# Key logarithms added to the decay exponents, and two VectorE steps moved to ScalarE, in the first mixer of a two-layer network

## What is computed

```python
xc = silu(causal_conv4(x, conv_w))
q, kg, v, g = xc @ wq, xc @ wkg, xc @ wv, xc @ wg + bg
gk = log_sigmoid(kg) / 16
k = 1 - exp(gk)
S = S * exp(gk_t) + k_t (x) v_t        # for each token and head
o_t = (q_t * scale) S
o = o + sigmoid(sum(q * aug * k) * v)
o = head_norm(o)
x1 = layernorm(x + silu(g) * o @ wout)
```

## Time and profile before

| what | value |
|---|---|
| median of 3 runs | 4582.89 us (4578.5 to 4586.45) |
| the profiled execution's own time | 4581.29 us |
| its span | 4579.3 us |
| mean granted TensorE clock | 0.924 |
| span of the first mixer, from the slices and the last logits' copy | 0 to about 860 us |
| busy in the whole span: PE, PEld, DVE, ACT, POOL | 87%, 67%, 54%, 43%, 24% |

### The profile page before, as it was taken

The page is one execution under the profiler, slowest core; times in us unless marked ns, Lnnn a source line. Parts: engine busy times, 40 slices in busy tenths (PEclk is TensorE's granted clock), DMA queues, the critical chain, the costliest instruction groups (busy, mean ns, idle before and its releaser), DMA issues. The chain is left out here.

```text
span 4579.3 us, 72621 instructions
## 1 busy us (share of the span) xinstructions
PE 3966.9 (87%) x23860; PEld 3077.2 (67%) x23860; DVE 2462.0 (54%) x5456; ACT 1990.2 (43%) x4069; POOL 1085.3 (24%) x1689
## 2 busy tenths in 40 slices
PE   5887788698999999993798888888888888769998
PEld 3555555377888888881576767676767677646666
DVE  7888888452222222224577777777777676421111
ACT  5655655111222222212466666666666566432222
POOL 0111111102222222212343333333333332200000
PEclk8888888799999999996799999999999999879999
DMA  1010010345555555552111111111111110011111
GB/s 34 29 42 28 28 42 20 75 135 179 183 183 183 184 183 185 183 170 68 39 42 40 43 41 42 42 42 38 42 43 42 42 42 25 20 51 55 55 55 46
DMA packets 220427, 345.91 MB, mean 76 GB/s; under 512 B 99956, under 2 KB 171380, under 8 KB 201972
## 3 DMA queue, kind: packets, MB, share of 16 engines
q1 hardware_dynamic: 196404, 271.69, 18.7%
q0 software_dynamic: 23760, 71.07, 4.9%
HBM read 275.56 MB, written 67.63 MB: 75 GB/s over the span
## 5 line engine op out<-in xcount | busy, mean ns | idle before, releaser
L525 ACT ACTIVATE moe_rel<-moe_fc 128x512 f32<-128x512 f32 x284 | 169.6, 597 | 798.5 <-PE moe_fc L490 798.5
L490 PE MATMUL moe_fc<-moe_xT,moe_win 128*128 128x256 f32 x2272 | 503.8, 380 | 1.5 <-issue 0.8
L501 PE MATMUL moe_o<-moe_wout,moe_hT 128*128 128x256 f32 x2272 | 502.0, 379 | 0.0
L490 PEld LDWEIGHTS moe_fc<-moe_xT,moe_win 128*128 128x128 f32 x2272 | 433.1, 191 | 60.8 <-issue 2.1
L501 PEld LDWEIGHTS moe_o<-moe_wout,moe_hT 128*128 128x128 f32 x2272 | 426.6, 190 | 54.8
L549 DVE TENSOR_TENSOR moe_hT<-moe_rel 128x512 f32<-128x512 f32 x284 | 196.7, 693 | 361.0 <-ACT moe_rel L525 361.0
L1776 DVE SCALAR_TENSOR_TENSOR gdr_y<-gdr_bank,gdr_cw,gdr_y 128x511 f32<-128x511 f32 (+2 forms) x384 | 287.5, 749 | 79.8 <-ACT gdr_y L2044 59.3
L2251 PE MATMUL gdr_bank<-gdr_hT,gdr_wqkv 128*128 128x512 f32 x512 | 261.7, 636 | 41.5 <-ACT gdr_qk L2059 24.6
L558 DVE COPY moe_osb<-moe_o 128x512 f32<-128x512 f32 x71 | 49.1, 692 | 424.9 <-PE moe_o L501 424.9
L723 DVE TENSOR_TENSOR ffn_z<-ffn_o,ffn_xres 128x512 f32<-128x512 f32 x32 | 20.6, 686 | 381.5 <-PE ffn_o L690 381.5
L679 PE MATMUL ffn_fc<-ffn_xT,ffn_win 128*128 128x512 f32 x512 | 224.5, 597 | 1.2 <-ACT ffn_xT L699 1.2
(11 more groups left out here) (391 smaller groups left out, 8584.6 us busy)
## 6 DMA issues: line engine op xcount, KB each, us to landing
moe_win<-in_moe_w SPq DMA_DIRECT2D x71, 1024.0 KB, 7.9
moe_wout<-in_moe_w SPq DMA_DIRECT2D x71, 1024.0 KB, 5.1
slots_out<-moe_osb POOLq DMA_DIRECT2D x71, 256.0 KB, 7.4
ffn_xin<-mixed_rows SPq DMA_DIRECT2D x17, 512.0 KB, 3.8
gla_xp<-in_xT_rows SPq DMA_DIRECT2D x16, 512.0 KB, 4.7
gla_xres<-in_x_rows SPq DMA_DIRECT2D x16, 512.0 KB, 3.9
token_rows<-gla_x POOLq DMA_DIRECT2D x16, 512.0 KB, 3.4
rt_W<-in_fc_b SPq DMA_DIRECT2D x32, 256.0 KB, 3.3
```

The costliest lines, as they stand in the source:

```text
L490: ins = nc.tensor.matmul(fc_ps[j][:, m % 2, :], win[u][:, c, m * P:(m + 1) * P], xT[:, c, :], start=(c == 0), stop=(c == DT - 1))
L501: ins = nc.tensor.matmul(o_ps[u][:, t, :], hT[u][:, k, t * P:(t + 1) * P], wout[u][:, k, :], start=(k == 0), stop=(k == FT - 1))
L525: nc.scalar.activation(rel[:, j, :, :], fc_ps[j][:], ACT.Relu).then_inc(relu_done, 1)
```

## The change

Three things are changed in `linear_attention`.

1. The logarithm of the keys. The nine products by k (L978 and the eight of L984) are gone. In their place DVE bounds k from below (`kc`), ACT takes its logarithm (`lk`), DVE subtracts G from it (`logk`), and the nine differences become sums of G_ref and `logk`. Their Exp then gives the keys already multiplied. `keys` and `scores(0)` on PE wait for ACT's exponents now instead of DVE's products.
2. The closing norm's scaling moves from DVE (L97, four instructions) to ACT (`normed`, four Identity activations with a scale and a bias for each row), and DVE makes only the bias (`shift`, 128x4). `normed` stands behind the value copies in ACT's queue and ahead of the `x1T` copies.
3. The convolution's first tap moves from DVE (L944) to ACT (`tap`, at the head of the body). DVE's other taps wait for it.

```diff
-                    link(ts(yc[:, c, :], xp[u][:, c, 0:L], cw[:, c, 0:1], None, ALU.mult))
+                    wait("tap", c + 1)
...
-                        done("D", 2, tt(khat[:], G[:, :, CH - 1:CH].broadcast_to([P, NCH, CH]), G[:], ALU.subtract))
...
-                            done("D", 3 + a, tt(kt[u][:, :, a, 0:n], G[:, :, r:r + 1].broadcast_to([P, NCH, n]), G[:, :, 0:n], ALU.subtract))
-
-                def products(part, b, u):
+                            done("D", 3 + a, tt(kt[u][:, :, a, 0:n], G[:, :, r:r + 1].broadcast_to([P, NCH, n]), logk[:, :, 0:n], ALU.add))
+
+                def logs(part, b):
                     wait, done = waiter(dve, b)
                     if part == 0:
...
                         wait("k", 1)
-                        wait("E", 3)
-                        done("khat", 1, tt(khat[:], khat[:], k_[:], ALU.mult))
-                        done("aw", 1, tt(aw[:], qs[:], flat(k_[:]), ALU.mult))
+                        done("kc", 1, ts(flat(k_[:]), flat(k_[:]), K_FLOOR, None, ALU.max))
                     else:
-                        for a in range(4 * (part - 1), 4 * part):
-                            n = SUB * (a + 1)
-                            wait("E", 5 + a)
-                            done("kt", a + 1, tt(kt[u][:, :, a, 0:n], kt[u][:, :, a, 0:n], k_[:, :, 0:n], ALU.mult))
+                        wait("lk", 1)
+                        Chain(dve, log_step, b)(tt(flat(logk[:]), ab[:], flat(G[:]), ALU.subtract))
+                        done("D", 2, tt(khat[:], G[:, :, CH - 1:CH].broadcast_to([P, NCH, CH]), logk[:], ALU.add))
...
+                        if later(b, 0):
+                            dve.wait_ge(s["x1"], b)
...
-                        dve.wait_ge(x1_free, b + 1)
                         wait("lnrstd", 1)
-                        done("x1", 1, row_scale(nc, z, x1, agg, rstd, TT))
+                        done("shift", 1, stt(shift[:], agg[:, :, 0], -1.0, rstd[:], ALU.mult, ALU.mult))
...
                         differences(0, b + 1, w)
-                        differences(1, b + 1, w)
+                        logs(0, b + 1)
                     if past is not None:
                         head_norm(2, past, w)
                         head_norm(3, past, w)
                     if more:
+                        logs(1, b + 1)
+                        differences(1, b + 1, w)
                         differences(2, b + 1, w)
...
+                def tap(b, u, turn):
+                    wait, done = waiter(act, b)
+                    act.wait_ge(x_in[u], turn * 16 + 16)
+                    for c in range(DT):
+                        done("tap", c + 1, a_op(yc[:, c, :], xp[u][:, c, 0:L], ACT.Copy, scale=cw[:, c, 0:1]))
...
+                        wait("kc", 1)
+                        done("lk", 1, a_op(ab[:], flat(k_[:]), ACT.Ln))
                         wait("D", 2)
...
+                def normed(b):
+                    wait, done = waiter(act, b)
+                    act.wait_ge(x1_free, b + 1)
+                    wait("shift", 1)
+                    for t in range(TT):
+                        ins = a_op(x1[:, t, :], z[:, t, :], ACT.Identity, scale=rstd[:, t:t + 1], bias=shift[:, t:t + 1])
+                    done("x1", 1, ins)
...
+                    if far is not None:
+                        tap(b + 2, u, far)
                     if more:
                         gates(b + 1)
...
                     if past is not None:
+                        normed(past)
                         turned(past, "x1Tp", "x1T", x1T)
...
-                        wait("kt", NSUB)
+                        wait("E", 4 + NSUB)
...
-                    wait("khat", 1)
+                    wait("E", 3)
```

More of the change, by code:

```diff
@@ L744 @@
 GK_FLOOR = -21.0
+K_FLOOR = 1e-35
 def linear_attention(nc, x_rows, xT_rows, conv_w, wq, wkg, wv, wg, bg, wout, aug_bal, w_gate, x1_rows, logits_out):
@@ L778, in linear_attention @@
         qhat, khat = two("qhat", [P, L]), sb("khat", [P, NCH, CH])
+        logk = sb("logk", [P, NCH, CH])
         S = sb("S", [P, NCH, D])
@@ L797, in linear_attention @@
         pKV, pO = ps("pKV", [P, 512]), ps("pO", [P, 512])
-        per = dict(conv=DT, xc=1, qk=1, abs=2, l1=1, q=1, gq=1, gg=1, D=2 + NSUB, ek=1, k=1, E=4 + NSUB, qt=1, qhat=1, khat=1, aw=1, kt=NSUB,
+        per = dict(tap=DT, conv=DT, xc=1, qk=1, abs=2, l1=1, q=1, gq=1, gg=1, D=2 + NSUB, ek=1, k=1, E=4 + NSUB, qt=1, qhat=1, kc=1, lk=1, aw=1,
                    spread=1, vg=TT, v=TT, sg=1, kdp=1, kd=2, augp=1, augr=1, av=1, sig=1,
                    sc=TT, A=TT, kv=TT, kvr=TT, S=NCH - 1, op=TT, o=TT,
-                   om=1, sq=1, var=1, rstd=1, on=1, oTp=1, oT=DT, y=2, z=2, lnvar=1, lnrstd=1, x1=1, x1Tp=1, x1T=DT, lgp=1, lg=1)
+                   om=1, sq=1, var=1, rstd=1, on=1, oTp=1, oT=DT, y=2, z=2, lnvar=1, lnrstd=1, shift=1, x1=1, x1Tp=1, x1T=DT, lgp=1, lg=1)
         s = {n: sem("s_" + n) for n in per}
@@ L806, in linear_attention @@
             "id0", "id1", "consts", "w_in", "xres_in", "x1_stored", "x1_free", "lg_stored", "lg_free", "set_up", "pool_step"))
-        gate_step, norm_step, tail_step, conv_step = (sem(n) for n in ("gate_step", "norm_step", "tail_step", "conv_step"))
+        log_step, gate_step, norm_step, tail_step, conv_step = (sem(n) for n in ("log_step", "gate_step", "norm_step", "tail_step", "conv_step"))
         def waiter(eng, b):
@@ L938, in conv @@
                     wait, done = waiter(dve, b)
-                    link = Chain(dve, conv_step, b * 6 + 3 * c)
-                    if c == 0:
-                        dve.wait_ge(x_in[u], turn * 16 + 16)
-                        if later(b, 0):
-                            dve.wait_ge(s["xc"], b)
-                    link(ts(yc[:, c, :], xp[u][:, c, 0:L], cw[:, c, 0:1], None, ALU.mult))
+                    link = Chain(dve, conv_step, b * 4 + 2 * c)
+                    wait("tap", c + 1)
                     for k in range(1, 4):
@@ L965, in differences, with products @@
                             n, r = SUB * (a + 1), SUB * a + SUB // 2 - 1
-                            done("D", 3 + a, tt(kt[u][:, :, a, 0:n], G[:, :, r:r + 1].broadcast_to([P, NCH, n]), G[:, :, 0:n], ALU.subtract))
-                def products(part, b, u):
+                            done("D", 3 + a, tt(kt[u][:, :, a, 0:n], G[:, :, r:r + 1].broadcast_to([P, NCH, n]), logk[:, :, 0:n], ALU.add))
+                def logs(part, b):
                     wait, done = waiter(dve, b)
                     if part == 0:
-                        wait("q", 1)
-                        wait("E", 1)
-                        done("qt", 1, tt(qt[:], flat(eR[:]), qs[:], ALU.mult))
-                        wait("E", 2)
-                        done("qhat", 1, tt(qhat[u][:], flat(eG[:]), qs[:], ALU.mult))
                         wait("k", 1)
-                        wait("E", 3)
-                        done("khat", 1, tt(khat[:], khat[:], k_[:], ALU.mult))
-                        done("aw", 1, tt(aw[:], qs[:], flat(k_[:]), ALU.mult))
-                    else:
-                        for a in range(4 * (part - 1), 4 * part):
-                            n = SUB * (a + 1)
-                            wait("E", 5 + a)
-                            done("kt", a + 1, tt(kt[u][:, :, a, 0:n], kt[u][:, :, a, 0:n], k_[:, :, 0:n], ALU.mult))
+                        done("kc", 1, ts(flat(k_[:]), flat(k_[:]), K_FLOOR, None, ALU.max))
+                    else:
+                        wait("lk", 1)
+                        Chain(dve, log_step, b)(tt(flat(logk[:]), ab[:], flat(G[:]), ALU.subtract))
+                        done("D", 2, tt(khat[:], G[:, :, CH - 1:CH].broadcast_to([P, NCH, CH]), logk[:], ALU.add))
+                def products(b, u):
+                    wait, done = waiter(dve, b)
+                    wait("q", 1)
+                    wait("E", 1)
+                    done("qt", 1, tt(qt[:], flat(eR[:]), qs[:], ALU.mult))
+                    wait("E", 2)
+                    done("qhat", 1, tt(qhat[u][:], flat(eG[:]), qs[:], ALU.mult))
+                    done("aw", 1, tt(aw[:], qs[:], flat(k_[:]), ALU.mult))
                 def own(b, u):
@@ L1080, in body @@
                     if more:
-                        products(0, b + 1, w)
+                        products(b + 1, w)
                     if past is not None:
                         tail(0, past)
-                    if more:
-                        products(1, b + 1, w)
                     if past is not None:
@@ L1090, in body @@
                         outputs(2, b, u)
-                    if more:
-                        products(2, b + 1, w)
                     if far is not None:
@@ L1215, in _ @@
                 act.wait_ge(set_up, 9)
+                tap(0, 0, 0)
                 silu(0, 0)
```

2 lines of the change are left out of this document (1 added, 1 removed).

## The result

The changed kernel takes 4742.92 us in the median of 6 runs (4731.83 to 4751.85), the kernel before, run beside it, 4584.67 us: ratio 1.0337, 95% interval 1.0317 to 1.0357. That is 158 us slower. The forecast was 74 us slower and a range up to 4694 us, so the direction is right and the size is wrong by a factor of two. The profiled execution of the changed kernel takes 4738.58 us.

What follows compares the result with a forecast made beforehand. PE's unbroken run behind z was taken as the bound, with DVE's chain ahead of z. 14 bodies at 4.9 us (68.6) + 7.2 + 0.8 - 2.5 = 74 us on 4581 gave 4655 us, range 4628 to 4694.

Steps and rivals of the forecast that it cites:

- What bounds the kernel: Mixer body: DVE's chain leads up to z; behind z PE runs without a gap, hiding DVE's work beside 13.4 us.
- The logarithm: Front half: kc, logk, gaps and waits bring DVE to masked(2) 1.8 us later, at 518.15.
- the next waiter: y, behind the state product and the oT copies: both lead to y at 520.2, against 518.40 before.
- The clock at y: PE's clock at y after 3.2 us idle: the values start 1.35 us late at full clock or 3.0 us at the lower.
- the slower bound: First half of y at 1.2 GHz costs 3.57 us, second back at 1.89; the values start 3.0 us late.
- 2.45 us of PE idle in each body: Before x1 is turned: PE waits for ACT's scaling behind the last value copy, turning x1 at 537.3 instead of 534.8.
- The loop starts: Five bodies where DVE stands still at the start of a loop turn: the moved tap gives back 5 x 0.5 us.
- DVE as the bound: Rival: the next body waits for DVE's work, so 6.1 us less a sequence, 92 us in all, 4490 us; chance 0.05.
- waits that cancel: Rival: ACT or PE finds hidden slack, so less than 0.6 us a body is lost; chance 0.03.
- The rival of the clock: Both halves of y and outputs(2) at the lower clock: values 6.0 us late, 8.5 us a body, 4706 us; chance 0.13.
- The rival of the table switch: At logk, a switch holds ACT 1.28 us beyond its load in 16 sequences: 20 us more, 4675 us; chance 0.07.

Runs made afterwards that it cites:

- the fillers: Changed kernel with three unread products in PE's wait before x1 and two more ahead of the state product: 4656.87 us, ratio 1.0151.
- The three filler products: Changed kernel with three unread 128x512 products in PE's idle time before x1 is turned: 4679.07 us, ratio 1.0204.
- the reordered version: Changed kernel without logarithm, scaling behind first value copy, squares ahead of gates, masked(2) earlier, khat and aw products behind z, oT copies earlier: 4550.19 us, ratio 0.9912.

## Why the prediction was wrong

**What bounds the kernel: right.** PE's run behind z was named as the bound and DVE's work there as worthless. The logarithm frees eight `kt` products on DVE and the kernel is slower by 50 us with it alone; the tap alone gives 1.0013. DVE now waits 10.6 us at `outputs(3)` (7 or 8 were forecast).

**The logarithm: its own terms right, the next waiter mis-sized.** `masked(2)` was forecast 14.2 us behind the variance and stands at 14.24. The state product was due 1.8 us late and comes at 492.46 - 476.71 = 15.75 us, where 13.91 stood before. But y starts 16.96 us behind the variance, not 16.25: the step let the `oT` copies follow DVE's last sum, while it is ACT's own chain, load, `khat` and 4.31 us of `kt` exponentials, that ends last, and y starts 0.7 us later than forecast. (The terms of that step, 518.1 + 0.63 + 1.2, also make 519.9 and not the 520.1 written.)

**The clock at y: beyond the slower bound.** The bounds were a first half of 1.94 and 3.57 us with the second back at 1.89, which gave 1.35 and 3.0 us. Measured: 3.30 and 1.89 in one body, 3.75 and 2.49 in the next. With the later start the front half costs 3.85 us instead of the 2.45 taken, and the fillers price the clock's part at 1.6 us a body.

**The step that failed: "2.45 us of PE idle in each body", and nothing behind it.** The idle time is 2.86 us by the trace and 2.92 by the table, since four activations take 2.07 us and not 4 x 0.417 = 1.67. That is 0.4 us a body. The large miss is that the term ended there. The forecast had seen that idle time ahead of y leaves the clock low, and even had a rival for it, but did not ask the same of the idle time that it had itself put before `x1`. There the clock is at its lower level in every second body for about 17 us, in the others for about 3, and the stretch to the next variance is 25.45 and 18.95 us where PE at the full clock needs 17.48. The three filler products give those 64 us back. What the miss adds up to: 1.4 us ahead of the values, 0.47 at `x1`, 3.86 behind it, 5.7 us a body, times 14 is 80 of the 84 us. The loop starts were right in direction and too small: 5 x 0.5 us was forecast to come back, and the whole stand of 15.5 us is gone, worth 14 x 0.7 = 10 us. The 3.86 us has this in it already.

**The rivals.** DVE as the bound (4490 us) and waits that cancel fell with the first runs. The rival of the clock (4706 us) had the right mechanism at the wrong place, y and `outputs(2)`; the values never started 6.0 us late. The rival of the table switch fell: ACT's activation starts 0.01 us behind the load, the second load starts 0.10 us behind the end of the logarithm, and a function that needs no table brings y forward by 0.36 us, where the rival wanted 1.28 us on top of the loads' own time. By this, the rule of the Trainium skill, ScalarE: Activation LUTs, section What ACT_TABLE_LOAD costs, that a switch adds a drain of about 1.38 us to the load, does not show here; its load of about 1.28 us does.

**A coincidence to note.** With the clock held at both places the changed kernel takes 4656.87 us and the forecast was 4655. They are not the same sum: the forecast counted about 1.1 us a body for the clock at y and left out 0.7 us of ACT's chain and 0.4 us of activations.

## What to carry to other kernels

Before moving work from one engine to another, find the consumer that waits last and ask at which place in the new engine's queue the work stands ahead of it; the same four activations cost 121 us behind the last value copy and nothing behind the first. When a sum contains new idle time on TensorE, price the work behind it at the lower clock as well: here, behind `x1`, that was 4.55 us a body for an idle time of 2.86. A few products that nobody reads, just long enough for the wait, show in one run how much of a loss is clock, and can be kept in the kernel. They help only where the next engine waits for PE: where PE itself goes on to wait for DVE, five of them held the clock up and shortened nothing.

## What the runs showed of the hardware

- An idle time of 2.86 us, at the same place behind the same work, has two outcomes in turn: the granted clock falls to its lower level and PE runs there for about 17 us although it is busy for nearly all of it (0.53 in 451.2 to 469.5 us; at levels of 0.5 and 1 that is 17.2 of the 18.3 us), or it is back within 3 us of the turning (outputs at 1.18 us from 516.68). The first turning behind the long one's idle time still runs at the full clock (0.65 us for four, against 1.11 behind the other). Why they alternate wasn't tried.
- DVE's stand at the start of a loop turn, 15.5 us in 5 times in the kernel before (the earlier trace rows shows one, 2.96 us), is also there with the tap alone (17.4 us) and with the scaling alone (15.3 us), and in none of the other kernels. A wait of the same engine shortly before doesn't decide it: with the scaling alone DVE waits 6.1 us at `outputs(3)` and stands still all the same, and in the reordered version it waits 0.8 us there and doesn't. The three kernels that have the stand are those with the most DVE instructions, 5408 to 5456 against 5376 or fewer. Whether that is the reason was not tried.
- A filler product 128x512 in f32 is two records and takes some 0.9 us at the full clock: 5.42 us for six, 4.45 for five, 2.84 for three.
- Four activations 128x256 with a scale and a bias for each row take 2.07 us, 0.52 each, where the exponentials of that shape took 0.417.
